# A head of an attention kernel with its statistics seven tiles ahead, and fewer VectorE operations per block

## What is computed

```python
def reference(x, wq_w, wq_b, wk_w, wk_b, wv_w, wv_b, wo_w, wo_b, w1, conv_w, conv_b, w2):
    # x: (8, 2048, 1024) float32, 16 heads of 64
    xn = layernorm(x)
    q, k, v = xn @ wq.T + bq, xn @ wk.T + bk, xn @ wv.T + bv
    s = where(xn[:, :, 0] != 0, q @ k.T * 64**-0.5, -inf)
    attn = (softmax(s) @ v) @ wo.T + bo
    # feed-forward: activations rounded to int8 steps per row, weights to -1, 0, 1
    h = act_quant(xn) @ weight_quant(w1).T          # 1024 -> 4096
    h = silu(depthwise_conv1d(h, conv_w, conv_b))   # 3 taps along the sequence
    return x + attn + act_quant(h) @ weight_quant(w2).T
```

## Time and profile before

| what | us |
|---|---|
| runs of the kernel before: lowest, median, highest of 3 | 1182.61, 1260.81, 1311.77 |
| the profiled execution, its own time | 1182.18 |
| span of its slowest core (core 1) | 1180.6 |
| spans of all eight cores | 1174.3 to 1180.6 |
| head and main loop of core 1, until the last exponential has ended | about 645 |

### The profile page before, as it was taken

How to read it: one execution, slowest core, us unless ns; L and a number is a source line. 1 busy time by engine, 2 the same in 40 slices (tenths; PEclk the granted TensorE clock), 3 DMA queues, 4 the chain that set the end, 5 groups by cost and what they waited for, 6 DMA issues and landing times.

```text
span 1180.6 us, 28483 instructions; the slowest of 8 cores (1174.3 to 1180.6 us)
## 1 busy us (share of the span) xinstructions
PE 1091.4 (92%) x9138; PEld 593.5 (50%) x9138; DVE 890.5 (75%) x1487; ACT 815.8 (69%) x1110; POOL 242.8 (21%) x263
## 2 busy tenths in 40 slices
PE   2679999999999999999988999989999999999998
PEld 2355655655565665655555444444444444444443
DVE  5437888988887888888851788877777777878866
ACT  3578888888888899899998545456666666556300
POOL 4220000000000000000012123233333333332684
PEclk9799999999999999999999999999999999999999
DMA  8535557555463767757673344574354545453452
GB/s 220 184 53 140 168 163 197 161 151 172 165 194 89 183 152 180 189 162 203 186 170 88 117 148 154 172 233 128 114 161 134 173 136 170 136 157 88 136 185 89
DMA packets 84061, 183.06 MB, mean 155 GB/s; under 512 B 24816, under 2 KB 28944, under 8 KB 83920
## 3 DMA queue, kind: packets, MB, share of 16 engines
q1 hardware_dynamic: 79248, 172.52, 48.3%
q0 software_dynamic: 4240, 8.69, 5.0%
q10 hardware_dynamic: 432, 0.04, 0.0%
HBM read 164.44 MB, written 25.17 MB: 161 GB/s over the span
## 4 chain that ended last, share of the span: by engine, by line
PE 67%; ACT 15%; issue 7%; DVE 7%; POOL 1%; DMA 1%; ACTq 0%; DVEq 0%; POOLq 0%; SPq 0%
PE psC L914 16%; PE psA L932 15%; ACT probs L405 14%; PE psS L500 11%; PE psV L517 5%; PE psQ L449 5%; PE psA L900 4%; PE psQ L465 3%; PE psQ L458 3%; PE psC L932 2%; DVE wsum L644 1%; DMA xhead<-x 1%; DVE u_sb L1067 1%; DMA strm<-x 1%; DVE xarea L1135 1%
## 5 line engine op out<-in xcount | busy, mean ns | idle before, releaser
L405 ACT ACTIVATE probs<-psS 128x1024 bf16<-128x1024 f32 x512 | 506.6, 1023 | 69.1 <-PE psS L500 52.7
L500 PE MATMUL psS<-qz,kroll 128*128 128x512 bf16 x1024 | 304.3, 378 | 18.7 <-ACT probs L405 14.0
L914 PE MATMUL psC<-xqT,w1q_sb 128*128 128x512 bf16 x1024 | 242.4, 381 | 0.0
L517 PEld LDWEIGHTS psV<-v_sb,probs 128*128 128x128 bf16 x4096 | 183.8, 97 | 77.9 <-issue 5.0
L932 PE MATMUL psA<-w2q_sb,hq 128*128 128x512 fp8e4 x896 | 212.6, 379 | 6.4 <-DVE hq L1118 6.2
L825 POOL TENSOR_TENSOR h_act<-h_act,shb_sb 128x512 f32<-128x512 f32 x128 | 165.4, 1296 | 229.0 <-DVE hq L1118 198.1
L517 PE MATMUL psV<-v_sb,probs 128*128 128x65 bf16 x4096 | 200.4, 194 | 1.7 <-DVE cn L633 0.6
L914 PEld LDWEIGHTS psC<-xqT,w1q_sb 128*128 128x128 fp8e4 x1024 | 99.1, 98 | 115.9 <-issue 1.9
L932 PEld LDWEIGHTS psA<-w2q_sb,hq 128*128 128x128 bf16 x896 | 87.0, 98 | 113.7 <-issue 10.8
L1067 DVE SCALAR_TENSOR_TENSOR u_sb<-psC,cws,u_sb 128x511 f32<-128x511 f32 x128 | 95.7, 748 | 62.0 <-ACT u_sb L850 61.9
L850 ACT ACTIVATE u_sb<-psC,cws 128x510 f32<-128x510 f32 (+2 forms) x128 | 87.5, 684 | 53.5 <-PE psX L924 52.3
(11 more groups left out here) (109 smaller groups left out, 1057.8 us busy)
## 6 DMA issues: line engine op xcount, KB each, us to landing
strm<-w_t SPq DMA_DIRECT2D x128, 512.0 KB, 4.7
w2q_sb<-w2q_stage SPq DMA_DIRECT2D x112, 256.0 KB, 2.6
w1q_sb<-w1q_stage SPq DMA_DIRECT2D x64, 256.0 KB, 3.1
xhead<-x SPq DMA_DIRECT2D x16, 512.0 KB, 7.1
strm<-x SPq DMA_DIRECT2D x16, 512.0 KB, 4.4
xarea<-x SPq DMA_DIRECT2D x16, 512.0 KB, 5.8
res_stage<-xarea SPq DMA_DIRECT2D x16, 512.0 KB, 3.1
xarea<-res_stage SPq DMA_DIRECT2D x16, 512.0 KB, 5.8
```

Source lines behind the costliest of these rows:

```text
L405: s.activation(out=probs[:, (i % NP) * 1024:(i % NP + 1) * 1024], in_=psS[:, b * 1024:(b + 1) * 1024], func=AF.Exp, scale=0.125, bias=-B0) ...
L500: mm = t.matmul(psS[:, b * 1024 + hh * 512:b * 1024 + (hh + 1) * 512], kTv[:, hp % 2, kc * 128:(kc + 1) * 128], qz[:, (it % 4) * 1024 + hh ...
L517: mm = t.matmul(psV[:, hh * 512 + qt * 65:hh * 512 + (qt + 1) * 65], probs[:, o:o + 128], v_v[:, kc, 2 * hp + hh, :], start=(kc == 0 and q ...
L914: mm = t.matmul(mbank(g), w1q_sb[:, o + cc * 256:o + cc * 256 + 128], xqTv[:, cc, tb * 512:tb * 512 + 512], start=(cc == 0), stop=(cc == N ...
```

## The change

Six things are altered. (1) DVE's statistics run seven tiles ahead of the evacuations and no longer five. (2) The first `q` job is at i = 5, the first scores at i = 6, the first exponential in ACT's iteration 7; `HS` is 10, and since step 10 now uses the score buffer that step 9 has, its scores also wait for exponential 9. (3) A `q` job is evacuated in one scalar_tensor_tensor: the bank is read twice by a repeated dimension, the bias added, and the result multiplied by a 128x2 mask of ones and zeros that is repeated along the columns; POOL writes this mask in four small memsets where it zeroed `qz`. (4) The `keep` column is copied for all 16 heads once per tile, by the head's `v` job; the 48 later `v` jobs have one operation. (5) `norm` has one reciprocal over eight columns. (6) The third part of an `x` tile has two operations and two waits where it had four and three. The planner's costs follow.

```diff
@@ -141,7 +142,7 @@
     NW = W1CH + W2CH
     NIT = NHP * NQB
     NSTEP = NIT * NT
-    HS = NT - 5
+    HS = NT - 6
 
 
     jobs = []
@@ -149,7 +150,7 @@
     for i in range(1, NT + 1):
         if i % 4 == 0:
             head_after[i].append(("k", 0, i // 4 - 1))
-        if i == 4:
+        if i == 5:
             head_after[i].append(("q", 0, 0))
         if i == 14:
             head_after[i].append(("q", 1, 0))
@@ -161,10 +162,10 @@
         strm_items += [("w", ch) for ch in range(4 * n, 4 * n + 4)] + [("x", n)]
     strm_items.insert(strm_items.index(("x", NT - 1)), ("m", 0))
     strm_items += [("gap", 0)] + [("z", ch) for ch in range(NW)]
-    part_us = {"w": [1.2], "x": [0.9, 1.2, 0.9, 1.8], "m": [0.3], "gap": [5.0],
+    part_us = {"w": [1.2], "x": [0.9, 1.2, 0.5, 1.8], "m": [0.3], "gap": [5.0],
                "z": [0.8, 0.8, 0.9]}
-    evac_us = {"k": 0.75, "q": 1.55, "v": 0.6, "t": 0.75, "x": 0.65, "m": 1.0}
-    norm_us = 1.5
+    evac_us = {"k": 0.75, "q": 1.2, "v": 0.5, "t": 0.75, "x": 0.65, "m": 1.0}
+    norm_us = 1.3
 
     n_pieces = {"k": 8, "q": 8, "v": 8, "t": 1, "x": 1, "m": 1}
     last_piece = {k: n - 1 for k, n in n_pieces.items()}
@@ -313,7 +314,11 @@
     WQST = 16 * (NW // 4)
 
     def a_gload(g):
-        g.memset(qz[:], 0.0).then_inc(sem("qz0"), 1)
+        for h in range(2):
+            for m in range(2):
+                g.memset(hmask[64 * m:64 * m + 64, h:h + 1],
+                         1.0 if h == m else 0.0).then_inc(sem("hmask"), 1)
+        g.wait_ge(sem("hmask"), 4)
         g.wait_ge(sem("x_l1"), 16)
         g.dma_start(out=wv_sb[:, 0:2048], in_=wv_d[0]).then_inc(sem("wv_l0"), 16)
         gv = [0]
@@ -410,10 +415,10 @@
             norm(i)
             if i >= 1:
                 tile_evac(i - 1)
-            if i >= 6:
-                exps(i - 6)
+            if i >= 7:
+                exps(i - 7)
         tile_evac(NT - 1)
-        for i in range(NT - 6, NSTEP):
+        for i in range(NT - 7, NSTEP):
             exps(i)
     on("scalar", a_scalar)
 
@@ -489,6 +494,7 @@
                 t.wait_ge(sem("p_e"), g)
             elif g == HS:
                 t.wait_ge(sem("ln_e"), 2 * NT)
+                t.wait_ge(sem("p_e"), HS)
             elif g > HS:
                 t.wait_ge(sem("p_e"), g - 1)
             b = 0 if g < HS else g % 2
@@ -523,13 +529,13 @@
         for i in range(NT + 1):
             if i < NT:
                 tile_transpose(i)
-            if i >= 7:
-                pv(i - 7)
+            if i >= 8:
+                pv(i - 8)
             for job in head_after[i]:
                 for p in range(8):
                     piece(job, p)
-            if i >= 5:
-                scores(i - 5)
+            if i >= 6:
+                scores(i - 6)
         for i in range(HS, NSTEP):
             if i + 1 < NSTEP:
                 scores(i + 1)
@@ -587,21 +593,25 @@
                                 OP.add).then_inc(sem("pq_ev"), 1)
             elif kind == "q":
                 hp, o = a // NQB, (a % 4) * 1024
-                if a == 0:
-                    v.wait_ge(sem("qz0"), 1)
                 if a >= 4:
                     v.wait_ge(sem("p_s"), NT * (a - 3))
-                v.tensor_scalar(qz[0:64, o:o + 512], ps[0:64, :], bqc[0:64, hp:hp + 1], None,
-                                OP.add)
-                v.tensor_scalar(qz[64:128, o + 512:o + 1024], ps[64:128, :],
-                                bqc[64:128, hp:hp + 1], None, OP.add).then_inc(sem("pq_ev"), 1)
+                if a == 0:
+                    v.wait_ge(sem("hmask"), 4)
+                v.scalar_tensor_tensor(
+                    qz[:, o:o + 1024].rearrange("p (h t) -> p h t", h=2),
+                    ps.unsqueeze(1).to_broadcast([128, 2, 512]), bqc[:, hp:hp + 1],
+                    hmask[:].unsqueeze(2).to_broadcast([128, 2, 512]),
+                    OP.add, OP.mult).then_inc(sem("pq_ev"), 1)
             elif kind == "v":
-                v.tensor_scalar(v_v[:, a, 4 * b:4 * b + 4, 0:64],
+                ev = v.tensor_scalar(v_v[:, a, 4 * b:4 * b + 4, 0:64],
                                 ps[:, 0:256].rearrange("p (h d) -> p h d", h=4),
                                 keep[:, a:a + 1], None, OP.mult)
-                v.tensor_copy(v_v[:, a, 4 * b:4 * b + 4, 64:65],
-                              keep[:, a:a + 1].unsqueeze(1).to_broadcast([128, 4, 1])
-                              ).then_inc(sem("pq_ev"), 1)
+                if b == 0:
+                    v.tensor_copy(v_v[:, a, :, 64:65],
+                                  keep[:, a:a + 1].unsqueeze(1).to_broadcast([128, H, 1])
+                                  ).then_inc(sem("pq_ev"), 1)
+                else:
+                    ev.then_inc(sem("pq_ev"), 1)
             elif kind == "t":
                 hp, qb = a // NQB, a % NQB
                 v.tensor_scalar(ctxv[:, hp, qb * 512:(qb + 1) * 512], ps, bvc[:, hp:hp + 1], None,
@@ -623,13 +633,11 @@
             v.wait_ge(sem("p_pv"), NT * (it + 1))
             if it >= 2:
                 v.wait_ge(sem("pq_pe"), jidx[("t", it - 2, 0)] + 1)
+            dep(v.reciprocal(rden[:].rearrange("p (h q) -> p h q", h=2),
+                             psV.ap().rearrange("p (h c) -> p h c", h=2)[:, :, 64:260:65]))
             for hh in range(2):
                 acc_v = psV[:, hh * 512:hh * 512 + 260].rearrange("p (q d) -> p q d", q=4)
-                dep(v.reciprocal(rden[:, 4 * hh:4 * hh + 4], acc_v[:, :, 64:65].rearrange(
-                    "p q d -> p (q d)")))
-            for hh in range(2):
-                acc_v = psV[:, hh * 512:hh * 512 + 260].rearrange("p (q d) -> p q d", q=4)
-                v.wait_ge(sem("dv"), dv[0] - 1 + hh)
+                v.wait_ge(sem("dv"), dv[0])
                 v.tensor_tensor(cnv[:, s2, :, hh * 64:(hh + 1) * 64], acc_v[:, :, 0:64],
                                 rden[:, 4 * hh:4 * hh + 4].unsqueeze(2).to_broadcast([128, 4, 64]),
                                 OP.mult).then_inc(sem("cn_w"), 1)
@@ -654,12 +662,10 @@
                     dep(v.reduce_max(tiny[:, 5:6], xt, axis=AX, apply_absolute_value=True))
                 elif part == 2:
                     v.wait_ge(sem("dv"), dv[0])
-                    dep(v.tensor_scalar(tiny[:, 6:7], tiny[:, 5:6], 1e-5, None, OP.max))
+                    dep(v.tensor_scalar(tiny[:, 7:8], tiny[:, 5:6], 1e-5, 1.0 / 127.0,
+                                        OP.max, OP.mult))
                     v.wait_ge(sem("dv"), dv[0])
-                    v.tensor_scalar(tiny[:, 7:8], tiny[:, 6:7], 1.0 / 127.0, None, OP.mult)
-                    dep(v.reciprocal(tiny[:, 8:9], tiny[:, 6:7]))
-                    v.wait_ge(sem("dv"), dv[0])
-                    dep(v.tensor_scalar(tiny[:, 9:10], tiny[:, 8:9], 127.0, None, OP.mult))
+                    dep(v.reciprocal(tiny[:, 9:10], tiny[:, 7:8]))
                 else:
                     v.wait_ge(sem("dv"), dv[0])
                     v.tensor_scalar(xt, xt, tiny[:, 9:10], meff[:, 0:1],
@@ -699,13 +705,13 @@
                                         sem("wqv"), 1)
                     v.engine_nop().then_inc(sem("sm_done"), 1)
 
-        for i in range(NT + 6):
+        for i in range(NT + 8):
             if i < NT:
                 stats(i)
-            if i == 5:
+            if i == 7:
                 v.wait_ge(sem("cstq"), 16 * 2)
-            if 5 <= i:
-                for job in head_after[i - 5]:
+            if 7 <= i:
+                for job in head_after[i - 7]:
                     evac(job)
         v.wait_ge(sem("cst"), CST)
         for i in range(HS, NSTEP):
```

More of the change, by code:

```diff
@@ L90, in _build @@
     mvv = mvar.ap().rearrange("p (t k) -> p t k", k=2)
+    hmask = E(nc.sbuf_tensor("hmask", [128, 2], F32))
     ln_w = E(nc.sbuf_tensor("ln_w", [128, 4 * 4], F32))
```

## The result

The changed kernel took 1164.3 us in the median (1162.0 to 1164.5, four runs); beside the kernel before the ratio is 0.985, 95% interval 0.984 to 0.986. That is 1.5% less time, so within the 2% that the prediction counts as no clear change.

What follows compares the result with a forecast made beforehand. Main loop bound by PE at first, then PE and ACT; in the head ACT waits for POOL's late scale and shift. 1182.2 - 12.6 (head) - 2.5 (main loop) = 1167.1 us; range 1154 to 1184.

Steps and rivals of the forecast that it cites:

- Sum: Whole kernel: 1182.2 us of the profiled execution less 12.6 and 2.5 gives 1167.1; runs' median 79 us above, not forecast.
- A term put at nothing: Main loop: the step that the head loses is done there in its stead, at no cost or gain.
- Seven tiles ahead: Head: earlier statistics end ACT's waits for POOL; norm(8) at 45, norm(12) at 58.4; head -12.6 us, bounds -5 and -16.
- The late q job: Head: the 2.0 us q job no longer stands before tile 4's last transposes (38.6 us); not priced apart from the head's walk.
- Operations: DVE, mainly main loop: q 1.27 us, x tile's third part 0.5, fewer small operations; some 17 us less DVE work.
- 2.5 us gained: Main loop: net of cheaper DVE operations, about half taken back by a denser stream; bounds 9 gained and 24 lost.
- Late loads: Head, rival: tile loads take twice as long, norm(8) at 49, norm(12) at 63 to 65; head -6, 1174 us; chance 0.17.
- sign of being wrong: Head: DVE waiting for `xhead` in the middle of the head would show the forecast wrong; no size given.
- Vanishing waits: Main loop, rival: PE's waits for DVE all but vanish, nine us gained, head -15; 1158 us; chance 0.11.
- Slow q: q evacuation on DVE, rival: one operation takes 2.0 us, costing 16 us of DVE; 1185 us; chance 0.04.
- The denser stream: Copies of 16 x tiles, steps 20 to 234, rival: PE waits 35 us for 10.9, +24; 1194 us; chance 0.06.

Runs made afterwards that it cites:

- the head's edits alone: Kernel before with only statistics seven tiles ahead, first q at i = 5, HS 10 and the added wait; operations and planner costs as before: ratio 0.988.
- The lag alone: Kernel before with only the statistics seven tiles ahead instead of five, q at i = 4 and HS 11 kept: ratio 0.991.

## Why the prediction was right or wrong

**The relation to the median failed.** The step is the paragraph "Sum". It starts from the profiled execution, 1182.2 us, and takes off 15.1 us, 1.3%; 1.5% came. Of the runs' median it says only that it is 79 us above and that no such run is forecast, and it gives 1167.1 as it stands. Beside that median, 1260.8, the number reads as a change of 7.4%, several times the measured one. What the runs showed in its place: the change is worth a ratio of 0.985 beside a time near 1182 us, and the 79 us are no part of it. A forecast of a change should have been carried by the ratio, 0.987, and not left to a level that the given median did not share. The time itself came out at 1164.3, 2.8 us below the forecast.

**A term put at nothing failed too.** "The step that the head loses is done in the main loop in its stead: nothing" left out that the planner starts from `HS`: the head's edits alone took 3.2 us off the main loop.

**Seven tiles ahead: right, step by step.** norm(4), norm(8) and norm(12) were put at 30.5, 45 and 58.4 us and came at 30.53, 44.84 and 57.94; the head at -12.6 us, measured -13.1. The terms came one by one on core 1: norm(12) 12.9 us earlier for 12.4, from there to the last k job 1.4 for 1.1, and from that job to the twelfth exponential 0.9 lost for 0.9. The lag alone gave 12.3, the sharpest confirmation that POOL waited for statistics queued behind an evacuation. The late q job, which I had only as part of the same walk, cannot be told from nothing in the head.

**Operations: durations right, their worth mis-sized.** q was put at 1.27 us and took 1.283; the third part at 0.5, took 0.53; some 17 us less work for DVE, and it was 17.6 in core 1's main loop. An estimate by the rule in the Trainium skill's "Vector Engine (DVE) Microarchitecture Reference", section 5.2, as I read it onto a repeated operand, was some 2.0; the 1283 ns say that a word repeated 512 times is read at full rate. But "2.5 us gained" for all of this had been thought of as some 5 us of gain, half taken back. The operations gave about 6, and the new costs took back 5.2 to 5.5, nearly all. With the 3.2 of `HS` the net is -3.9, near the forecast partly by luck: two terms were mis-sized in opposite directions.

**The rivals.** Late loads: DVE did wait for `xhead` in the middle of the head, 2.02 us. The prediction had named this as a sign of being wrong, and it was not, since PE had a job in hand. Vanishing waits: they did not vanish in the changed kernel; with the old costs they fell to 3.1 us on core 0, and that kernel came to 1159 us. Slow q: refuted. The denser stream: the new placement does cost, at the evacuations as foreseen, but 5 us and not 24, and it was outweighed; that density is the reason is not shown.

## What to carry to other kernels

When an in-order engine serves both a producer far ahead and consumers, ask of each queued item what it waits for, and put the producer's work ahead of any item that waits for its own result; the right lead can be read from the queue's order. When operations get cheaper, change a planner's costs in a run of their own: here honest new costs moved its placement and lost nearly all that the cheaper operations had gained, and the old costs were faster than either kernel. Shifts of a few steps were worth as much as the operations, 3 to 5 us either way, and nothing here foretells their sign: try several placements. And state a forecast as a ratio to an execution that is named.

## What the runs showed of the hardware

A scalar_tensor_tensor that reads a bank of 512 columns twice by a repeated dimension, with a 128x2 mask repeated 512 times in each half, takes 1283 ns for 1024 columns, 535 ns above the 748 of 511 columns: one column in 1.04 ns, repeated or not.

The clock fell where I had expected it to hold. In the kernel with tiles 4 to 7 in two groups the last idle stretch of PE before the second k job was 1.63 us on core 4, and the job took 3.27 us at a granted clock of 0.58; core 6, with the same 1.63 us, and core 1, with 1.82, did it in 1.89. With the statistics six tiles ahead, 2.94 to 2.95 us of idling were followed by 1.89 us on core 2, 2.60 on core 1 and 3.60 on core 5. So neither the length of that stretch nor one core's trace tells whether the clock will fall. What decides it, these runs do not show; to see what it costs, look at all eight cores.
